# Batch 0 of a cross-attention: ScalarE evicts the scores, VectorE takes the maximum and writes all low parts

## The reference

```python
bf = einsum('bqd,kd->bqk', layernorm(x), w1_w) + w1_b
scores = einsum('bqd,bkd->bqk', bf, ctx) / sqrt(256)      # 4096 keys in each batch
attn = softmax(scores, axis=-1)
output = einsum('bqk,bkd->bqd', attn, ctx)
x = x + concat([layernorm(x), output]) @ w2_w.T + w2_b
```

## Time and profile before

| | |
|---|---|
| median of 3 runs | 600.28 us (600.08 to 600.31) |
| the profiled execution | 599.96 us, its span 598.2 us |
| TensorE busy | 571.6 us (96%) |
| VectorE busy | 414.6 us (69%) |
| ScalarE busy | 332.5 us (56%) |
| GpSimd busy | 254.5 us (43%) |
| mean granted TensorE clock | 0.989 of 2.4 GHz |

### The profile page before, as it was taken

One profiled execution on the slowest core, in us unless ns is written; L12 is line 12 of the kernel. 1 busy time (PEld: TensorE's weight loads), 2 busy tenths in 40 slices (PEclk: granted clock), 3 DMA queues, 4 the chain that ended last, 5 costly groups with the idle time before them and its releaser, 6 DMA issues.

```text
span 598.2 us, 9977 instructions
## 1 busy us (share of the span) xinstructions
PE 571.6 (96%) x3765; PEld 487.6 (82%) x3765; DVE 414.6 (69%) x701; ACT 332.5 (56%) x564; POOL 254.5 (43%) x259
## 2 busy tenths in 40 slices
PE   7799999999999999989999989999999999999995
PEld 5589988998799889967676867888888888888884
DVE  3866686668656865579888688676767676777761
ACT  4337535753476455628766827565647474747450
POOL 6366347534742484334544620333333333333212
PEclk9999999999999999999999989999999999999998
DMA  8993086008600200000002966999999999999642
GB/s 291 424 413 157 1 329 233 1 2 324 239 1 2 71 1 2 1 1 1 2 2 75 397 260 240 339 323 342 332 345 329 339 333 354 337 343 323 226 154 88
DMA packets 25166, 119.27 MB, mean 199 GB/s; under 512 B 2640, under 2 KB 8912, under 8 KB 14096
## 3 DMA queue, kind: packets, MB, share of 16 engines
q1 hardware_dynamic: 20752, 112.48, 49.9%
q0 software_dynamic: 4368, 6.16, 5.3%
HBM read 113.52 MB, written 6.42 MB: 200 GB/s over the span
## 4 chain that ended last, share of the span: by engine, by line
PE 80%; DVE 11%; ACT 2%; issue 2%; POOL 2%; DMA 2%; POOLq 0%; SPq 0%; DVEq 0%; ACTq 0%
PE psum L1653 20%; PE psum L1430 14%; PE psum L1670 13%; PE psum L1384 12%; PE psum L1290 11%; PE psum L1346 2%; DVE head_max L963 2%; DVE region_a L968 1%; DMA region_w<-ctx_cols_dram 1%; PE psum L1528 1%; POOL wide_low L562 1%; DVE wide_low L985 1%; PE psum L1312 1%; PE psum L1392 1%; PE psum L1502 1%
## 5 line engine op out<-in xcount | busy, mean ns | idle before, releaser
L677 ACT ACTIVATE wide_high<-region_a 128x1024 fp32r<-128x1024 f32 (+1 forms) x104 | 105.2, 1011 | 97.7 <-PE psum L1653 90.2
L1120 DVE TENSOR_TENSOR wide_low<-region_a,wide_high 128x1024 fp32r<-128x1024 f32 x92 | 112.4, 1224 | 58.2 <-ACT wide_high L677 58.2
L1670 PE MATMUL psum<-region_a,region_w 128*128 128x256 f32 x368 | 83.3, 379 | 0.0
L1430 PE MATMUL psum<-turned_high,wide_low 128*128 128x256 f32 x256 | 78.6, 307 | 2.9 <-DVE turned_low L1046 2.4
L1046 DVE TENSOR_TENSOR turned_low<-psum,turned_high 128x512 fp32r<-128x512 f32 x64 | 43.7, 690 | 54.2 <-ACT turned_high L677 54.1
L1653 PE MATMUL psum<-wide_low,turned_high 128*128 128x512 f32 x184 | 78.2, 425 | 0.2 <-DVE turned_high L1222 0.2
L1670 PEld LDWEIGHTS psum<-region_a,region_w 128*128 128x128 f32 x368 | 69.7, 190 | 10.0
L1653 PE MATMUL psum<-wide_high,turned_low 128*128 128x512 f32 x184 | 72.5, 394 | 0.0
L1430 PE MATMUL psum<-turned_high,wide_high 128*128 128x256 f32 x256 | 72.2, 282 | 0.0
L1430 PE MATMUL psum<-turned_low,wide_high 128*128 128x256 f32 x256 | 72.1, 282 | 0.0
L1653 PE MATMUL psum<-wide_high,turned_high 128*128 128x512 f32 x184 | 72.1, 392 | 0.0
(11 more groups left out here) (223 smaller groups left out, 1196.3 us busy)
## 6 DMA issues: line engine op xcount, KB each, us to landing
region_a<-up_weights_dram SPq DMA_DIRECT2D x23, 2048.0 KB, 9.1
region_a<-down_weights_dram SPq DMA_DIRECT2D x23, 1024.0 KB, 7.3
region_w<-ctx_cols_dram SPq DMA_DIRECT2D x32, 512.0 KB, 9.3
region_a<-ctx_dram SPq DMA_DIRECT2D x16, 1024.0 KB, 12.2
third_weights<-third_weights_dram SPq DMA_DIRECT2D x1, 1035.0 KB, 26.0
residual<-x_dram SPq DMA_DIRECT2D x4, 256.0 KB, 7.8
sums_by_token<-residual SPq DMA_DIRECT2D x2, 512.0 KB, 9.5
normed_rows<-region_s SPq DMA_DIRECT2D x4, 256.0 KB, 6.6
```

The lines of the kernel that those rows point to most:

```text
L677: return nc.scalar.activation(dst, src, ACT.Copy)
L1120: nc.vector.tensor_tensor(w_lo[:, k % RING], group_of(k), w_hi[:, k % RING].bitcast(F32), ALU.subtract).then_inc(low_ready, 1)
L1430: last = nc.tensor.matmul(bank[6 + c][:, 0:NTOK], v[:, value_slot(b, g), k, c * P:(c + 1) * P], p[:, g % 2, k, :], start=g == 0 and k == 0 ...
L1670: last = nc.tensor.matmul(to[:, 0:D], hidT[n][:, ic * P:(ic + 1) * P], rows, start=ic == 0, stop=ic == IC - 1)
```

## The change

- `ON_POOL[0]` is empty: VectorE writes all low parts of batch 0's context chunks.
- The scores of chunks 0 to 6 of batch 0 are evicted by ScalarE (`scores_evicted`), two instructions for a chunk, issued behind `ctx_out(ch + 3)`; those of chunks 5 and 6 come behind the loop. VectorE takes the maximum of both tiles in one reduction over the evicted scores, and waits for it. Chunk 7 stays as it was.
- The square root for batch 1's rows moves from ScalarE to GpSimd, and ScalarE loads the table for Exp before the first chunk instead of between chunks 3 and 4.
- In batches 0 and 1 the late rows are normalised one at step 9 and one at step 11.

```diff
-LATE_STATS, LATE_ROOT, LATE_NORM, LATE_TURN, LATE_COPY = 4, 10, 9, 12, 14
+LATE_STATS, LATE_ROOT, LATE_NORM, LATE_TURN, LATE_COPY = 4, 10, [9, 11], 12, 14
-ROOT_FIRST, ROOT_SECOND = [0, 0, 1, 3], [2, 4, 5, 6]
+ROOT_FIRST, ROOT_SECOND = [0, 1, 2, 4], [3, 5, 6, 7]
+ACT_EVICTS = CHUNKS - 1
-ON_POOL = [[1, 3, 5], [2, 4, 6], [2, 4, 6], [2, 4, 6]]
+ON_POOL = [[], [2, 4, 6], [2, 4, 6], [2, 4, 6]]
...
+                if b == 0:
+                    root(1, FIRST_AT[1], ROOT_FIRST[1])
                 for ch in ON_POOL[b]:
...
             deviation(0)
+            nc.scalar.activation(act_pause[:, 1:2], zeros[:, 0:1], ACT.Exp)
             setup_copy(0)
...
+                    def scores_evicted(ch):
+                        for t in range(TPB):
+                            act.wait_ge(scores_done, ch * TPB + t + 1 + FIRST)
+                            nc.scalar.activation(scores[t][:, ch * BANK:(ch + 1) * BANK], score_bank(ch, t), ACT.Copy,
+                                                 scale=float(D) ** -0.5).then_inc(scores_out, 1)
...
                         ctx_out(ch)
                         if b == 0 and ch == 0:
                             queries_high_part(0)
-                        if b == 0 and ch == SPLIT:
-                            deviation(1)
-                            act.wait_ge(consts, N_CONST)
-                            nc.scalar.activation(act_pause[:, 1:2], zeros[:, 0:1], ACT.Exp)
+                        if b == 0 and ch >= SPLIT:
+                            scores_evicted(ch - SPLIT)
...
                     if b == 0:
+                        for ch in range(CHUNKS - SPLIT, ACT_EVICTS):
+                            scores_evicted(ch)
+                        act.wait_ge(consts, N_CONST)
                         setup_copy(1)
...
-            def normalise(s):
+            def normalise(s, rows=None):
...
-                if s < 2:
+                if s == 0:
...
-                for t in range(2 * s, 2 * s + 2):
+                for t in rows or range(2 * s, 2 * s + 2):
...
-                        for t in range(TPB):
+                        if b == 0 and ch < ACT_EVICTS:
+                            dve.wait_ge(scores_out, (ch + 1) * TPB + FIRST)
+                            both = region_s[:, :].rearrange("p (t k) -> p t k", t=TPB)[:, :, ch * BANK:(ch + 1) * BANK]
+                            then(nc.vector.tensor_reduce(cmax[:, :, ch], both, axis=X_AXIS, op=ALU.max))
+                        for t in range(TPB if b > 0 or ch >= ACT_EVICTS else 0):
...
-                        if b < 2 and g == LATE_NORM:
-                            normalise(b + 2)
+                        if b < 2 and g in LATE_NORM:
+                            at = (b + 2) * TPB + LATE_NORM.index(g)
+                            normalise(b + 2, range(at, at + 1))
```

## The result

The changed kernel takes 600.54 us (median of 20 runs, 598.70 to 602.51), the kernel before in runs beside it 599.23 us (596.51 to 600.46). The ratio is 1.0026, with a 95% interval of 1.0015 to 1.0037: 1.6 us slower (0.9 to 2.2), just beyond the 0.2% that I took for no change. The profiled execution of the changed kernel has a span of 598.3 us and a mean granted clock of 0.986.

What follows compares the result with a forecast made beforehand. TensorE, busy 96% of the span, was taken as the bound. Score stage +2.9 (1.45 later starts, 1.4 low clock) and late rows -2.6 gave +0.3 on 599.96; with 0.3 from profile to median, 600.6 us, range 598.8 to 602.6.

Steps and rivals of the forecast that it cites:

- rival A: Batch 0's score stage: the clock falls twice, after each long gap; net +1.4 us, 601.7 us; chance 0.2.
- the likeliest case: Whole kernel with one fall of TensorE's clock: 600.6 us, own range 599.8 to 601.4; chance 0.45.
- The late rows: Batches 0 and 1: normalising one row at step 9, one at 11 recovers 1.30 us each, -2.6 us.
- the chain: Batch 0: ScalarE's high part and evictions, VectorE's reduction and low part wait in turn; chunk 7 starts 1.45 us later.
- the clock's fall: Batch 0's score stage: TensorE drops once to 1.2 GHz, slowing about seven matmuls of chunk 4; 1.4 us.
- first round: Up to chunk 2 of batch 0: it starts at 20.47 against 19.57; the gap grows from 2.0 to 2.9 us.
- the sum: Start times added link by link at full clock: chunk 2 at 20.47, chunk 4 at 28.87, chunk 6 at 36.58.
- Second and third round: Chunks 4 and 6 of batch 0: TensorE waits 2.7 us before chunk 4, about 1.6 us before chunk 6.
- Rival B: Before chunk 6, GpSimd's subtraction goes first and VectorE's low part waits 1.3 us; 601.9 us; chance 0.13.
- Rival C: Batch 0's chunks: steps take less time than reckoned and the clock stays up; 599.1 us, or 598.5; chance 0.18.
- Rival D: Late rows of batches 0 and 1 give nothing back, another wait takes over; 603.2 us; chance 0.04.
- What I treated as free: Moved Exp table load, root on GpSimd and SP's loads cost nothing; 0.3 us if the table load did not fit.

Runs made afterwards that it cites:

- late_only: The kernel before with only the late rows normalised one at step 9 and one at step 11: 596.76 us, ratio to before 0.9958.
- warm_after: The changed kernel with spare matmuls of zeros on TensorE ahead of its waits for chunks 2 and 4: 598.48 us, ratio to before 0.9996.
- no_late: The changed kernel with both late rows normalised at step 9 again: 602.92 us, ratio to before 1.0066.
- max_later: The changed kernel with the reduction of chunk c behind the low part of chunk c+2 instead of ahead of it: 589.88 us, ratio to before 0.9853.
- low_on_pool: The changed kernel with the low parts of chunks 1, 3 and 5 back on GpSimd: 607.16 us, ratio to before 1.0126.

## Why the prediction came out as it did

The time, 600.5 us, lies at the forecast of 600.6, but that closeness is luck: the kernel before measured 599.2 in the later runs, and not the 600.3 that the forecast started from. The honest measure is the difference: +0.3 us was forecast, +1.6 by the ratio (0.9 to 2.2) and +1.3 by the medians was measured. That is the size of rival A (+1.4), not of the likeliest case, and just outside the 1.2 us on either side that I had given the largest chance (0.50). The late rows and the chain came out as forecast; the step that was off is the price of the clock's fall, 1.4 us where it cost 2.4 to 2.5.

- *Late rows, -2.6:* right. late_only has -2.5 us. The first row took 0.76 us beside GpSimd's copy and the second 0.41 alone; both fit the step.
- *The chain, first round:* right. The gap before chunk 2 was forecast at 2.9 and is 2.90; the reduction was taken at 1.21 and takes 1.22; chunk 2 starts 8.63 us behind chunk 0, forecast 8.65 (20.47 less 11.82). All three rounds of the sum, which was worked out at the full clock, are borne out by warm_after: 8.60, 8.41 and 7.72 us from even chunk to even chunk, forecast 8.65, 8.40 and 7.71.
- *Second and third round:* 2.7 and 1.6 were forecast as gaps. They are 2.35 (2.63 in no_late) and 1.53. The first of them is shorter because chunk 3, which covers a part of the chain, began at the low clock and took longer. Chunk 4 itself starts 10.83 us behind chunk 2, 2.4 us more than the 8.40 of the sum, and that is the clock.
- *The clock's fall:* the mechanism was right, the size wrong. I expected one fall "as before" and priced it at 1.4 us, for about seven matmuls that start 0.43 us apart, as if it began inside a chunk; a whole chunk has twelve, so the sentence that all of chunk 4 is slow and its price did not fit each other. The fall began within the gap, and lasted through all twelve matmuls of chunk 2: 5.50 us against 3.02, so 2.5 us. With 2.5 in the place of 1.4 the sum gives 1.45 + 2.5 = 3.95 for the stage, which is what was measured (32.81 less 28.86), and +1.35 in all. That it agrees to the last digit says little, as it compares one profiled execution with another.
- *Rival A* (two falls) did not happen: one fall in each profile, behind the first gap in the changed kernel and behind the second in no_late. That one longer fall cost as much as my two.
- *Rival B* (GpSimd first before chunk 6) did not happen. VectorE's low part starts at 37.03, GpSimd's subtraction at 37.17, and it takes 2.24 us as in the earlier trace rows. The margin was 0.14 us.
- *Rival C* (faster): the chain was not shorter. warm_after shows what the changed kernel takes when the clock stays up, as C had it: 0.9996 (0.9973 to 1.0019), where C had 599.1, 0.2% less than before.
- *Rival D* falls with late_only.
- *The reductions themselves* took 1.22 us each, as forecast. That a tensor_reduce is to be expected in the slowest mode is what the Trainium skill says (VectorE: DVE Perf Modes, "Rules for kernel authors"); the trace agrees in so far as 1.22 us is also what the low part takes, a subtraction of the same size. But max_later has the same seven reductions and is 10 us faster: what cost was their place in the queue.
- *What I treated as free* was free: the table load ended before batch 0's transposes were done, ScalarE still waiting 0.27 us. But I did not see that the root's place on GpSimd would matter to anyone who puts work behind it (low_on_pool).

What is open: the two profiled executions differ by 0.1 us (spans of 598.3 and 598.2 us), while the medians differ by 1.3. Where the first block ends the changed kernel is 0.8 us late (its last products with w2T start at 261.4, against 260.6 before), and by the end of the span 0.7 us of this is gone, in the blocks that the change does not touch. I did not look for the reason.

## What to carry to other kernels

Before giving a step to another engine, write down the loop that it closes: here the high part of chunk c+3, the eviction and the reduction of chunk c and the low part of chunk c+2, over two engines, 7.7 us from the start of chunk 4 to that of chunk 6 (30.61 to 38.32), where TensorE alone needs 5.9 us for its matmuls and transposes (22.87 to 28.80, the same two starts in max_later). Put what the bottleneck waits for ahead of what nobody waits for: moving a reduction one place back in VectorE's queue was worth 10 us, six times what the change had cost. And take the good half: freeing VectorE from its neighbour GpSimd was right, and was hidden by the new order.

## What the hardware showed that I had not expected

- The length of a low-clock stretch is not fixed: 3.4 us in the kernel before, from 28.6 to 32.0, and 6.7 us in the changed one, from 18.9, while TensorE stood still, to 25.6. With the same score stage it followed the first gap (2.90 us) in the changed kernel's profile and the second (2.63 us) in that of no_late. Gaps of 2.03 us in the kernel before and of 2.92 us in no_late passed without a fall, and one of 2.23 us in the kernel before did not.
- A GpSimd instruction of two columns was held about as long as a big one beside a VectorE instruction that reads two operands from SBUF: it took 1.07 us instead of 0.20, where the subtraction of 128x512 took 2.24 instead of 1.29. GpSimd's timeline in the changed kernel, first beside VectorE's low part of 18.53 to 19.72, then the same line for later rows, while VectorE works on L1028, which reads one of its two tensors from PSUM:

```profile
18.70 1.07 POOL L530 TENSOR_TENSOR ln_sd<-ln_mean_var,eps 128x2 f32<-128x2 f32 x1 [10.08 <-DVE ln_mean_var L923]
...
60.12 0.20 POOL L530 TENSOR_TENSOR ln_sd<-ln_mean_var,eps 128x2 f32<-128x2 f32 x1
```
